# Store slots for the input terms of a recurrence, the place of their evictions, and the order of two weight loads

## What is computed

```python
x = x + attn(cond_attn(x, cond))     # two attentions, output projection, residual
h = cond                             # initial state of a GRU, one row per sequence
for t in range(256):                 # GRU over the tokens
    gi = x[:, t] @ W_ih + b_ih       # 3 * 512 columns: r, z, n
    gh = h @ W_hh + b_hh
    r = sigmoid(gi_r + gh_r); z = sigmoid(gi_z + gh_z)
    n = tanh(gi_n + r * gh_n)
    h = (1 - z) * n + z * h
    hs[:, t] = h
# mixture of 8 experts, top 2 per token, hidden size 352
scores = hs @ gate_w.T + gate_b + bias
comb = softmax weights of the two highest scores, 0 elsewhere
y_e = silu(hs @ w1_e.T + b1_e) @ w2_e.T + b2_e
out = x + sum over e of comb_e * y_e
```

## Time and profile before

| what | us |
|---|---|
| median of three runs | 2062.74 (2058.96 to 2065.62) |
| profiled execution, its own time | 2065.38 |
| its span, first to last instruction | 2063.5 |
| TensorE busy with matmuls | 1901.0 |
| VectorE busy | 1344.4 |
| ScalarE busy | 977.0 |
| POOL busy | 126.8 |

### The profile page before, as it was taken

The page is one execution under the profiler, slowest core; times in us unless marked ns, Lnnn a source line. Parts: engine busy times, 40 slices in busy tenths (PEclk is TensorE's granted clock), DMA queues, the critical chain, the costliest instruction groups (busy, mean ns, idle before and its releaser), DMA issues.

```text
span 2063.5 us, 80896 instructions
## 1 busy us (share of the span) xinstructions
PE 1901.0 (92%) x34632; PEld 1651.2 (80%) x34632; DVE 1344.4 (65%) x5145; ACT 977.0 (47%) x3438; POOL 126.8 (6%) x213
## 2 busy tenths in 40 slices
PE   5899999999999788778799999999999999999999
PEld 3677676776776577667789999899899898998988
DVE  4477767876776754334576777767766767777664
ACT  2354543654455454444454455444544544544443
POOL 1121020120210201011000000000000000000000
PEclk9899999999999899999899999999999999999999
DMA  7011010010110223233100000000000000000000
GB/s 277 23 45 44 1 44 32 13 44 1 44 44 1 94 79 102 81 111 105 57 19 4 25 23 18 14 19 19 14 19 19 29 4 29 19 19 14 4 13 11
DMA packets 55561, 81.53 MB, mean 40 GB/s; under 512 B 5616, under 2 KB 42352, under 8 KB 54688
## 3 DMA queue, kind: packets, MB, share of 16 engines
q1 hardware_dynamic: 50912, 64.79, 9.3%
q0 software_dynamic: 4288, 11.55, 1.9%
HBM read 61.09 MB, written 15.24 MB: 37 GB/s over the span
## 4 chain that ended last, share of the span: by engine, by line
PE 66%; DVE 17%; DMA 6%; ACT 5%; issue 3%; DVEq 1%; POOL 0%; ACTq 0%; SPq 0%; POOLq 0%
PE ps L1338 25%; PE ps L1292 10%; PE ps L1271 10%; PE ps L539 4%; DMA gi_d<-shared 4%; PE ps L537 3%; PE ps L573 3%; PE ps L547 2%; DVE mx L771 2%; PE ps L612 1%; ACT shared L1432 1%; PE ps L584 1%; PE ps L1259 1%; PE ps L558 1%; DMA shared<-in_W_hh 1%
## 5 line engine op out<-in xcount | busy, mean ns | idle before, releaser
L1338 PEld LDWEIGHTS ps<-nxt,whp 128*128 128x128 f16 x24576 | 648.6, 96 | 88.8 <-DVE nxt L1565 81.3
L1338 PE MATMUL ps<-nxt,whp 128*128 128x32 f16 x24576 | 657.5, 177 | 66.0 <-DVE nxt L1565 63.3
L1412 ACT ACTIVATE rz<-s,sc 128x32 f32<-128x32 f32 x512 | 164.1, 321 | 443.7 <-DVE s L1528 443.1
L1271 PE MATMUL ps<-cur,w1p 128*128 128x256 f16 x2112 | 272.1, 274 | 0.0
L1292 PE MATMUL ps<-shared 128*128 128x256 f16 x2112 | 265.8, 273 | 0.0
L1292 PEld LDWEIGHTS ps<-shared 128*128 128x128 f16 x2112 | 205.6, 98 | 23.7
L1271 PEld LDWEIGHTS ps<-cur,w1p 128*128 128x128 f16 x2112 | 198.4, 98 | 22.4
L1528 DVE TENSOR_REDUCE s<-ps 128x32 f32<-128x64 f32 x512 | 114.7, 224 | 139.1 <-PE ps L1338 137.7
L539 PE MATMUL ps<-kz,rot 128*128 128x256 f32 x512 | 156.4, 388 | 0.0
L1388 ACT ACTIVATE ps<-gi,sc 128x64 f32<-128x64 f32 x512 | 152.6, 298 | 0.1
L1553 DVE SCALAR_TENSOR_TENSOR dh<-nn,sc,h 128x32 f32<-128x32 f32 x256 | 64.5, 252 | 110.7 <-ACT nn L1412 93.3
(11 more groups left out here) (214 smaller groups left out, 2919.8 us busy)
## 6 DMA issues: line engine op xcount, KB each, us to landing
gi_d<-shared SPq DMA_DIRECT2D x84, 128.0 KB, 2.4
gi<-gi_d SPq DMA_DIRECT2D x14, 768.0 KB, 5.0
seen<-in_w1T SPq DMA_DIRECT2D x8, 704.0 KB, 4.0
seen<-in_w2T SPq DMA_DIRECT2D x8, 704.0 KB, 5.3
shared<-in_w1T POOLq DMA_DIRECT2D x20, 256.0 KB, 3.1
xall<-in_x SPq DMA_DIRECT2D x4, 1024.0 KB, 8.3
x1T<-in_xT SPq DMA_DIRECT2D x1, 4096.0 KB, 21.8
shared<-in_w2T POOLq DMA_DIRECT2D x16, 256.0 KB, 3.8
```

The lines of the kernel that those rows point to most:

```text
L1271: last = nc.tensor.matmul(ps[:, 6 + n % 2, 0:TT], w1p[:, k, wp, i * P:(i + 1) * P], cur[:, k, hq, :, :].rearrange("p s b -> p (s b)"), sta ...
L1338: last = nc.tensor.matmul(ps[:, bank, g * WIDE * 2 * B:(g + 1) * WIDE * 2 * B], whp[:, k, w, q, g * P:(g + 1) * P], h, start=False, stop=( ...
L1412: nc.scalar.activation(o.rearrange("p g b -> p (g b)"), i_.rearrange("p g b -> p (g b)"), func, scale=scale).then_inc(done, 1)
```

## The change

The stores of input terms get four slots in place of two: the two in `shared`, and two that are the halves of `small.b2`. `d_st` becomes four semaphores, and each wait on them is counted over four. As b2 is overwritten, it is loaded again after the last store: VectorE clears the tile at step 32, SP then issues three loads, and the splitting moves from steps 34 and 35 to 36 and 37. Of the two or three evictions of a step the first stays ahead of the tanh; the others are issued in `beside_first_tile`, behind the seeds and ahead of the x and weight pieces. The loads of W_ih and W_hh are issued in the last batch ahead of the slices j = 2 and 3 in place of behind them.

```diff
+                def load_gru_weights():
+                    sp.wait_ge(c_hb, B)
+                    sp.wait_ge(p_qk, 2 * B)
+                    sp.dma_start(shared[:, WI_AT:WI_AT + KD * G3]..., ins["W_ih"]...).then_inc(d_wi, 16)
+                    sp.wait_ge(p_v, B + 1)
+                    sp.dma_start(shared[:, WH_AT:WH_AT + KD * G3]..., ins["W_hh"]...).then_inc(d_wh, 16)
                 for b in range(B):
                     for j, (_, src, width) in enumerate(to_see(ins, b)):
+                        if b == B - 1 and j == 2:
+                            load_gru_weights()
                         if b or j >= 2:
                             sp.wait_ge(v_seen, 4 * b + j - 1)
                         sp.dma_start(seen[:, j % 2, 0:width], src).then_inc(d_seen[j % 2], 16)
-                sp.wait_ge(c_hb, B)
-                ...
-SMALL_AT = {1: 0, 2: 5, 3: 10, 4: 15, SPT + 2: 18, SPT + 3: 20}
+SMALL_AT = {1: 0, 2: 5, 3: 10, 4: 15, SPT + 4: 18, SPT + 5: 20}
-    stage = shared[:, STAGE_OFF:STAGE_OFF + 2 * TT].rearrange("p (j n) -> p j n", j=2)
+    stage = [shared[:, STAGE_OFF:STAGE_OFF + TT], shared[:, STAGE_OFF + TT:STAGE_OFF + 2 * TT],
+             small.b2[:, 0:TT], small.b2[:, TT:2 * TT]]
@@ SP
-                                     stage[:, u % 2, :]).then_inc(d_st[u % 2], 16)
+                                     stage[u % 4]).then_inc(d_st[u % 4], 16)
                     if now % (SPT // 2) == SPT // 2 - 1:
-                        for j in range(2):
-                            sp.wait_ge(d_st[j], 16 * NQ // 2)
+                        for j in range(4):
+                            sp.wait_ge(d_st[j], 16 * NQ // 4)
                         load_when_read(0, now // (SPT // 2))
                 sp.wait_ge(p_gi, UNITS)
                 sp.dma_start(sel32, ins["table"][:, T_ALL:]).then_inc(d_sel, 16)
+                sp.wait_ge(v_b2, 1)
+                for j in range(3):
+                    sp.dma_start(b2[j * NE:(j + 1) * NE, :], ins["b2"]).then_inc(d_b2, 16)
@@ ScalarE
                 def evict(u):
                     act.wait_ge(p_gi, u + 1)
-                    if u >= 2:
-                        act.wait_ge(d_st[u % 2], 16 * (u // 2))
+                    if u >= 4:
+                        act.wait_ge(d_st[u % 4], 16 * (u // 4))
...
                 def beside_first_tile(now):
+                    for u in here(EVICT_AT, now)[1:]:
+                        evict(u)
...
                 def first_gap(now):
-                    for u in here(EVICT_AT, now):
+                    for u in here(EVICT_AT, now)[:1]:
                         evict(u)
@@ VectorE
-                    if now == SPT + 2:
+                    if now == SPT:
+                        for j in range(4):
+                            dve.wait_ge(d_st[j], 16 * UNITS // 4)
+                        nc.vector.memset(b2[:, :], 0.0).then_inc(v_b2, 1)
+                    if now == SPT + 4:
+                        dve.wait_ge(d_b2, 48)
                         link(nc.vector.tensor_scalar(b2[:, :], b2[:, :], ...
-                    if now == SPT + 3:
+                    if now == SPT + 5:
                         link(tt(b2[:, :], b2[:, :], b2h, ALU.subtract))
```

More of the change, by code:

```diff
@@ L458, in _ @@
                     sp.dma_start(small.b2[j * NE:(j + 1) * NE, :], ins["b2"]).then_inc(d_small, 16)
+                def load_gru_weights():
+                    sp.wait_ge(c_hb, B)
+                    sp.wait_ge(p_qk, 2 * B)
+                    sp.dma_start(shared[:, WI_AT:WI_AT + KD * G3].rearrange("p (k n) -> p k n", k=KD),
+                                 ins["W_ih"].rearrange("(k p) n -> p k n", p=P)).then_inc(d_wi, 16)
+                    sp.wait_ge(p_v, B + 1)
+                    sp.dma_start(shared[:, WH_AT:WH_AT + KD * G3].rearrange("p (k n) -> p k n", k=KD),
+                                 ins["W_hh"].rearrange("(k p) n -> p k n", p=P)).then_inc(d_wh, 16)
                 for b in range(B):
                     for j, (_, src, width) in enumerate(to_see(ins, b)):
+                        if b == B - 1 and j == 2:
+                            load_gru_weights()
                         if b or j >= 2:
@@ L1159, in gru_and_ffn @@
         a_gi = sem(st, "a_gi")
-        d_st = [sem(st, "d_stage0"), sem(st, "d_stage1")]
+        d_st = [sem(st, f"d_stage{j}") for j in range(4)]
+        v_b2 = sem(st, "v_b2_zero")
+        d_b2 = sem(st, "d_b2")
         d_ws = [sem(st, f"d_wring{j}") for j in range(WRING)]
@@ L1208, in _ @@
                     if t < NT - 1:
-                        if t < 3:
-                            for j in range(2):
-                                sp.wait_ge(d_st[j], 16 * UNITS // 2)
+                        if t < 2:
+                            for j in range(4):
+                                sp.wait_ge(d_st[j], 16 * UNITS // 4)
                         for half in range(2):
@@ L1429, in evict @@
                     act.wait_ge(p_gi, u + 1)
-                    if u >= 2:
-                        act.wait_ge(d_st[u % 2], 16 * (u // 2))
-                    nc.scalar.activation(stage[:, u % 2, :], ps[:, 4 + u % 4, 0:TT], ACT.Identity,
+                    if u >= 4:
+                        act.wait_ge(d_st[u % 4], 16 * (u // 4))
+                    nc.scalar.activation(stage[u % 4], ps[:, 4 + u % 4, 0:TT], ACT.Identity,
                                          bias=bsum[:, u % NQ:u % NQ + 1], scale=sc[:, S_UNX:S_UNX + 1])\
@@ L1514, in _ @@
                         act.wait_ge(v_sm, SMALL_FIRST)
-                        for j in range(2):
-                            act.wait_ge(d_st[j], 16 * UNITS // 2)
+                        for j in range(4):
+                            act.wait_ge(d_st[j], 16 * UNITS // 4)
                     second_gap(now)
```

## The result

The changed kernel takes 2006.2 us (median of 4 runs, 2005.3 to 2009.2) where the kernel before, beside it on the same chip, takes 2062.1 (4 runs, 2059.0 to 2065.6). The ratio is 0.9727, 95% interval 0.9713 to 0.9741: 55.8 us less. The forecast was 2010, with a range of 1998 to 2033. The profiled execution took 2005.3 us, span 2003.5, against 2063.5 before; of these two executions one lies high and the other low in its own scatter, so their spans are 60.0 us apart.

The account below looks back on a forecast made before the run. ScalarE's waits for stores to land were taken to hold the first tile's steps, with TensorE the bound next. First tile -51.8, loads -2.0 and bias +0.7 sum to -53.1 us, from 2062.74 to 2009.6, said as 2010; range 1998 to 2033.

Parts of the forecast that it names:

- TensorE bounds a step without the store wait: First tile's 30 steps: TensorE busy throughout, 6.35 us with six half units, 5.69 with five, 182.6 us together.
- The 62.4 us go: First tile: ScalarE's 22 waits for a store to land before evicting into a slot, 62.4 us, all vanish.
- What comes on top: Step 1 to 32: additions of 1.5, 6 and 3 us to 187.2, giving 197.7 in place of 249.5.
- (c): Weight pieces outside the five tight steps, landing late for ScalarE's conversion: 3 us, ends 0 and 20.
- (b): Three-place weight ring: in steps 2, 7, 12, 19, 24 a place is freed only in the same step; 6 us.
- (a): First six half units of the recurrence, behind the pauses of step 0, keep their slow start: +1.5 us.
- The loads, -2.0 us: Recurrence's start: earlier W_ih and W_hh gain TensorE 1.4 and ScalarE 0.6 us; -2.0, ends -1 and -5.6.
- b2 as slots 2 and 3, +0.7 us: Step 32: VectorE clears the tile before the reload, 0.5, plus a little waiting: +0.7 us, 0 to 2.
- The first (the ring takes over, 2028): First tile: all 29.4 us of weight waits stay, or the clock stays at 0.91; about 2028 us; chance 0.21.
- The third (no change): Weight ring landings of 7 us would keep the old step of 8 us; 2058 to 2066 us; chance 0.04.
- The second (2001): Conversions hide wholly and nothing is given back: gain 60 to 64 us, 2001 us; chance 0.08.
- The fourth: Slower: stores land later with more traffic, evictions waiting for slots hold the next sigmoid; 2085 us; chance 0.03.

Follow-up runs that it names:

- less_pe_even_ring: The changed kernel without one of three products in the input terms' half units, and with the weight pieces spaced evenly over the steps: 1968.2 us, ratio 0.9540.
- less_pe_after: The changed kernel without one of three products in the half units (input terms of tiles 1 to 7): 1989.9 us, ratio 0.9634.
- slots_alone: The kernel before with four slots and the reloaded bias only; evictions and loads keep their old places: 2007.5 us, ratio 0.9726.
- move_alone: The kernel before with two slots and only the later evictions of a step moved behind the seeds: 2012.9 us, ratio 0.9754.
- even_ring: The changed kernel with the 46 weight pieces spaced evenly, one and two in turn, over the steps: 2003.0 us, ratio 0.9702.
- loads_alone: The kernel before with only the new place of the loads of W_ih and W_hh: 2064.8 us, ratio 0.9996.
- less_pe_before: The kernel before without one of three products in the half units (input terms of tiles 1 to 7): 2051.3 us, ratio 0.9931.
- ring_and_scales: The changed kernel with weight pieces spaced evenly and the scales' transposition ahead of the recurrence's first products: 1999.1 us, ratio 0.9674.

## Why the prediction came true, and where it was off

*TensorE bounds a step without the store wait.* Right, and the term that carries the sum. Regular steps take 6.33 and 5.67 us (6.35 and 5.69 were put in), and less_pe_even_ring shows the bound: with a third of the half units' matmuls away, 33.4 of 36.6 us come back once the ring is even. With the old ring (less_pe_after) about half came back: behind TensorE the ring comes next.

*The 62.4 us go.* Right in the sum; what the text left open is which part does it. It argued the slots and the move as one item, and asked of the waits only under four slots. slots_alone gives 0.9726 and move_alone 0.9754, where both give 0.9727: two cures of one wait, not two gains. The slots make the wait vanish; the move leaves 28.0 us of it in a place where all but some 5 us is hidden. With four slots the move brought nothing that the comparison can tell.

*What comes on top* was put too high: 197.7 us were forecast for step 1 to 32 and 191.07 measured. (c), other pieces of the ring, 3 us put in, was 0: three pieces outside the five crowded steps are waited for, 0.7 to 0.9 us, and hold no step. (b), the five crowded steps with 6 us: counted over each crowded step and those that catch up behind it, steps 2 to 4 lost 0.5, 7 and 8 nothing, 12 and 13 0.6, 19 and 20 1.5, 24 and 25 1.3, in all 3.9; by even_ring the ring is worth 3.6. The working behind it holds to the tenth: in step 19 the conversion starts at T+9.17 (863.50 to 872.67; T+9.1 was put in) and the next sigmoid comes 2.2 us late. (a), the first half units, 1.1 in place of 1.5, and step 31 4.16 in place of 4.6. Together with 0.02 us less in each regular step that makes up the 6.6 us of difference.

*The loads, -2.0 us.* This is the term that failed. The time of loads_alone, 0.9996 (0.9988 to 1.0005), just leaves room for 2.0 us; the traces don't: from table load to step 1 it takes 33.56 us where it took 34.28. The text took TensorE's earlier start of 1.4 us for a gain at the pace of before; the products then run at half the clock for longer, and end 0.1 us (loads_alone) to 0.3 us sooner. ScalarE's 0.6 us is there only on the mean: from table load to split, four kernels with the loads in their old place take 10.14 to 11.09 us (before, slots_alone, move_alone, less_pe_before) and five with the new place and the old order of the scales 9.21 to 10.55. It is too small to be told in the time. SP issued W_ih at 622.8 us and W_hh at 668.6, not both near 670, so the loads had landed long before they were wanted. That VectorE's scales would hold ScalarE next was seen; that they'd be hardly sooner was not. The loads' place became worth something only with the scales moved too (29.99 in place of 33.88 us from table load to step 1).

*b2 as slots 2 and 3, +0.7 us.* Too high. The clearing is

```profile
947.64 0.48 DVE L1639 MEMSET b<- 128x512 f32 x1
948.15 0.97 SPq L1214 DMA_DIRECT2D b<-in_b  x3
```

and step 32 takes 4.80 us where it took 4.64: 0.2 us. The 0.5 us for the clearing itself was right; most of it lies beside other work.

*Sum.* Between the profiled executions: -58.4 in the first tile, -1.0 ahead of it, -0.6 behind it, in all -60.0; the medians say -55.8, the forecast -53.1. The 4 us between the first two are scatter of single executions (2059.0 to 2065.6 before). Part of it lies ahead of the recurrence: the four kernels that start as the changed one does (it, even_ring, less_pe_after, less_pe_even_ring) begin step 1 at 752.4 to 756.0 us. So the -1.0 there can't be put down to the loads. That the medians end 2.7 us from the forecast is partly luck: the first tile's 6.6 us too little gain stands against the loads' too much and against that scatter.

*The rivals.* The first (the ring takes over, 2028) was refuted by 3.6 us of ring cost; with shorter steps (less_pe_after) it comes true. The third (no change) falls with the ratio. The second (2001) needed the ring's cost and part of the start to go as well, and ring_and_scales, which removes them, is at 1999. The fourth's wait shows in one step of move_alone, at two slots and behind a reload; landings that lengthen with traffic, which it needs, don't show. Its own figures (270 us instead of 242, on 2062.7) give about 2091 and not 2085.

## What to carry to other kernels

Before adding up parts, ask which of them remove the same wait: buffers alone were enough here and a later place in an engine's program nearly so, and the sum was right only because they had been priced as one. Read the bound that remains from a step that doesn't stall, and price what then falls behind by how often the same place of a ring is freed and refilled within one step. A load that lands sooner gains nothing while another input of its reader comes at the same time, so move both or none.

## What the runs showed of the hardware

The first products after the attention ran at a clock of 0.50 until 724 us, both when they began at 719.7 and when they began at 721.6, after pauses of 3.30 and 5.09 us: 16 products took 6.69 and 5.16 us, so an earlier start was worth 0.3 us at their end and not 1.9.

The store landings didn't lengthen with traffic. The medians were 2.6, 2.9 and 1.8 us at a DMA share of 0.30 to 0.31 (before, loads_alone, less_pe_before), 2.0, 1.9 and 2.6 at 0.38 (changed kernel, move_alone, slots_alone), and, in less_pe_even_ring at 0.47, 2.1, where the longest of the view, 6.0, is a reload of gi and the longest store took 4.9:

```profile
DMA to landing us min/median/max: 1.7/2.1/6.0
```

In move_alone and in the changed kernel the only stores over 4.0 us (7.1 and 5.6; 5.4) were issued 1.7 to 3.6 us behind a reload of 768 KB on the same queue.

The two weight loads took 11.3 and 20.4 us to land when SP issued them 0.4 us apart in the kernel before, and 10.0 and 10.3 when issued apart. The view of DMA issues (last column: us to landing), before and after:

```profile
shared<-in_W_ih SPq DMA_DIRECT2D x1, 3072.0 KB, 11.3
shared<-in_W_hh SPq DMA_DIRECT2D x1, 3072.0 KB, 20.4
```

```profile
shared<-in_W_ih SPq DMA_DIRECT2D x1, 3072.0 KB, 10.0
shared<-in_W_hh SPq DMA_DIRECT2D x1, 3072.0 KB, 10.3
```
